# Bias, exponential and s made over both banks of q at once (1024 columns) in tiles 7 to 14 of a retrieval-attention and dense kernel

## What is computed

```
xn  = layernorm(x)
q   = xn @ Wq.T + bq              (one head in four is used: 8 heads x 128 = 1024 columns)
s   = elu(q) + 1                  (= max(q, 0) + exp(min(q, 0)))
a   = s / (sum over the head of s*z + 1e-6)
out = x + (a @ M per head, repeated over 4 heads) @ Wo.T  +  xn @ (w * w_scale) + b
```

## Time and profile before

| | |
|---|---|
| Time, median of 3 runs | 243.72 us (243.49 to 243.82) |
| The profiled execution | 243.56 us, of which the span of the trace is 241.7 us |
| PE busy | 234.1 us, 97% of the span |
| DVE, ACT, POOL busy | 178.0, 119.6 and 108.4 us |
| TensorE clock granted | full speed in every slice |

### The profile page before, as it was taken

One profiled execution on the slowest core, in us unless ns is written; L12 is line 12 of the kernel. 1 busy time (PEld: TensorE's weight loads), 2 busy tenths in 40 slices (PEclk: granted clock), 3 DMA queues, 4 the chain that ended last, 5 costly groups with the idle time before them and its releaser, 6 DMA issues.

```text
span 241.7 us, 3385 instructions
## 1 busy us (share of the span) xinstructions
PE 234.1 (97%) x1030; PEld 186.7 (77%) x1030; DVE 178.0 (74%) x266; ACT 119.6 (49%) x276; POOL 108.4 (45%) x108
## 2 busy tenths in 40 slices
PE   8699999998999999999999999999999999999995
PEld 2488788885776788888888888888888888788885
DVE  2889695897998669887687694958666778995631
ACT  2654626628648923655463526455463747341110
POOL 1058734756271815553434326263403629657500
PEclk9999999999999999999999999999999999999999
DMA  7999999999370211424252515221212223244441
GB/s 225 405 417 411 383 242 225 216 217 217 94 252 5 53 51 52 127 54 126 53 168 53 161 50 169 52 91 42 88 52 73 56 75 108 76 136 136 133 174 44
DMA packets 21985, 34.83 MB, mean 144 GB/s; under 512 B 5200, under 2 KB 13136, under 8 KB 20816
## 3 DMA queue, kind: packets, MB, share of 16 engines
q1 hardware_dynamic: 19344, 26.63, 33.4%
q0 software_dynamic: 1376, 6.82, 13.4%
q10 hardware_dynamic: 1248, 1.18, 1.8%
HBM read 22.02 MB, written 4.19 MB: 108 GB/s over the span
## 4 chain that ended last, share of the span: by engine, by line
PE 33%; issue 31%; POOL 18%; DVE 8%; SPq 4%; DMA 2%; ACT 2%; ACTq 1%; POOLq 0%; DVEq 0%
POOL e_and_sz L313 9%; POOL xT L288 5%; PE attn_ps L793 4%; PE attn_ps L794 4%; PE attn_ps L795 4%; SPq L219 4%; POOL x L321 3%; PE q_ps L793 3%; PE q_ps L795 3%; PE q_ps L794 3%; DVE aT_lo L654 2%; PE dense_ps L793 2%; PE dense_ps L795 2%; PE dense_ps L794 2%; DMA xT<-in_xT 2%
## 5 line engine op out<-in xcount | busy, mean ns | idle before, releaser
L313 POOL TENSOR_TENSOR e_and_sz<-s,z_b 128x512 f32<-128x512 f32 x32 | 42.0, 1340 | 40.3 <-DVE den L633 40.2
L441 ACT ACTIVATE s<-s,rden 128x128 f32<-128x128 f32 x128 | 39.2, 389 | 40.5 <-DVE rden L637 40.5
L793 PE MATMUL attn_ps<-P_hi,aT_hi 128*128 128x512 f32 (+1 forms) x128 | 49.8, 389 | 0.5 <-DVE aT_lo L654 0.5
L795 PE MATMUL attn_ps<-P_hi,aT_lo 128*128 128x512 f32 (+1 forms) x128 | 49.1, 383 | 0.0
L794 PE MATMUL attn_ps<-P_lo,aT_hi 128*128 128x512 f32 (+1 forms) x128 | 49.0, 383 | 0.0
L793 PE MATMUL q_ps<-WqT_hi,xT_hi 128*128 128x512 f32 x104 | 42.1, 405 | 0.3 <-DVE s L628 0.3
L795 PE MATMUL q_ps<-WqT_hi,xT_lo 128*128 128x512 f32 x104 | 40.6, 390 | 0.0
L794 PE MATMUL q_ps<-WqT_lo,xT_hi 128*128 128x512 f32 x104 | 40.5, 389 | 0.0
L288 POOL TENSOR_TENSOR xT<-xT,mean_b 128x512 f32<-128x512 f32 x13 | 18.3, 1408 | 37.8 <-ACT mean_b L390 31.2
L621 DVE SCALAR_TENSOR_TENSOR q_ps<-q_ps,rstd,bq_b 128x512 f32<-128x512 f32 x28 | 21.0, 753 | 19.3 <-PE q_ps L795 19.3
L793 PEld LDWEIGHTS attn_ps<-P_hi,aT_hi 128*128 128x128 f32 x128 | 24.1, 188 | 6.2 <-issue 0.9
(11 more groups left out here) (82 smaller groups left out, 365.3 us busy)
## 6 DMA issues: line engine op xcount, KB each, us to landing
x<-in_WoT POOLq DMA_DIRECT2D x6, 1024.0 KB, 10.6
x<-in_x SPq DMA_DIRECT2D x16, 256.0 KB, 3.9
xT<-in_xT SPq DMA_DIRECT2D x16, 256.0 KB, 4.1
aT<-s SPq DMA_DIRECT2D x124, 32.0 KB, 1.9
out<-x SPq DMA_DIRECT2D x15, 256.0 KB, 2.3
MT<-s SPq DMA_DIRECT2D x96, 32.0 KB, 1.9
x<-in_WoT SPq DMA_DIRECT2D x2, 1024.0 KB, 14.0
s<-in_WqT SPq DMA_DIRECT2D x2, 512.0 KB, 7.1
```

The costliest lines, as they stand in the source:

```text
L313: nc.gpsimd.tensor_tensor(sz_eps[:, :, h * D // 2:(h + 1) * D // 2].rearrange("p g (j c) -> p j g c", j=2), by_quarter(sbuf_s[:, t % SRING ...
L441: last = nc.scalar.activation(a_g, a_g, ACT.Copy, scale=rden[:, t % 2, g:g + 1])
L793: nc.tensor.matmul(out, x_hi, w_hi, start=start, stop=False)
L795: return nc.tensor.matmul(out, x_lo, w_hi, start=False, stop=stop)
```

## The change

The four q banks become one PSUM tensor, whose banks lie side by side. For tiles 7 to 14 one instruction of 1024 columns takes the place of two of 512 for the bias, for each of the two steps of the exponential, and for s. These instructions wait for both halves of q. The places of the other work in the loops move with this: `xT_hi` on ACT comes behind both steps of the exponential instead of between the halves, `xT_lo` on DVE ahead of all of s instead of between its halves, and `moments` ahead of the bias. In step 7 the splits of P come ahead as well. Tile 15 keeps its two halves. PE, POOL and SP keep their lists.

```diff
-        q_ps = [bank(f"q{i}_ps") for i in range(4)]
+        q_banks = ctx.enter_context(nc.psum_tensor("q_ps", [P, 4, 512], F32))
+        q_ps = [q_banks[:, i, :] for i in range(4)]
...
+        def both_banks(t):
+            return q_banks[:, 2 * (t % 2):2 * (t % 2) + 2, :].rearrange("p h n -> p (h n)")
...
+            def exp_of_both(t):
+                act.wait_ge(q_biased, 2 * t + 2)
+                act.wait_ge(s_ready, 2 * t)
+                nc.scalar.activation(ebuf, both_banks(t), ACT.Relu, scale=-1.0).then_inc(qneg_ready, 2)
+                act.wait_ge(qneg_ready, 2 * t + 2)
+                nc.scalar.activation(ebuf, ebuf, ACT.Exp, scale=-1.0).then_inc(exp_ready, 2)
...
             for t in range(LEAD, T):
-                exp_of(t, 0)
-                if t + 1 < T:
-                    copy_xT_hi(t + 1)
                 if t == LEAD:
                     copy_P_hi(6)
-                exp_of(t, 1)
-                if t == LEAD:
                     copy_P_hi(7)
+                if t < T - 1:
+                    exp_of_both(t)
+                    copy_xT_hi(t + 1)
+                else:
+                    exp_of(t, 0)
+                    exp_of(t, 1)
                 copy_aT_hi(t - LEAD + 1)
...
+            def add_bias_to_both(t):
+                dve.wait_ge(rstd_ready, t + 1)
+                dve.wait_ge(q_filled, 2 * t + 2)
+                nc.vector.scalar_tensor_tensor(both_banks(t), both_banks(t), rstd[:, t:t + 1], bq_b[:], ALU.mult, ALU.add
+                                               ).then_inc(q_biased, 2)
+
+            def make_both_s(t):
+                dve.wait_ge(exp_ready, 2 * t + 2)
+                if t >= SRING:
+                    dve.wait_ge(aT_in[in_MT(t - SRING)], aT_landed(t - SRING))
+                nc.vector.scalar_tensor_tensor(sbuf_s[:, t % SRING, :], both_banks(t), 0.0, ebuf, ALU.max, ALU.add
+                                               ).then_inc(s_ready, 2)
...
             for t in range(LEAD, T):
-                add_bias(t, 0)
                 if t == LEAD:
                     split_P_lo(5)
                 if t + 2 < T:
                     moments(t + 2)
-                add_bias(t, 1)
                 if t == LEAD:
                     split_P_lo(6)
-                if t == LEAD:
                     split_P_lo(7)
-                turn_blocks(t - BEHIND - 1)
-                if t == LEAD:
+                if t < T - 1:
+                    add_bias_to_both(t)
+                    turn_blocks(t - BEHIND - 1)
                     split_xT_lo(t + 1)
-                make_s(t, 0)
-                if LEAD < t < T - 1:
-                    split_xT_lo(t + 1)
-                make_s(t, 1)
+                    make_both_s(t)
+                else:
+                    add_bias(t, 0)
+                    add_bias(t, 1)
+                    turn_blocks(t - BEHIND - 1)
+                    make_s(t, 0)
+                    make_s(t, 1)
                 split_aT_lo(t - LEAD + 1)
```

More of the change, by code:

```diff
@@ L95, in q_bank @@
             if t < LEAD and t % 3 == 1:
-                return attn_ps[h]
+                return attn_ps[h][:]
             return q_ps[2 * (t % 3 == 2 if t < LEAD else t % 2) + h]
+        def both_banks(t):
+            return q_banks[:, 2 * (t % 2):2 * (t % 2) + 2, :].rearrange("p h n -> p (h n)")
         def last_attn_ps(c):
-            return [attn_ps[(T - 1) % 2], q_ps[0]][c][:, 0:HID // 2]
+            return [attn_ps[(T - 1) % 2][:, 0:HID // 2], q_ps[0][:, 0:HID // 2]][c]
         x_in = [sem(f"x_in{t}") for t in range(T)]
@@ L427, in exp_of @@
                 e = ebuf[:, halves(h)]
-                nc.scalar.activation(e, q_bank(t, h)[:], ACT.Relu, scale=-1.0).then_inc(qneg_ready, 1)
+                nc.scalar.activation(e, q_bank(t, h), ACT.Relu, scale=-1.0).then_inc(qneg_ready, 1)
                 act.wait_ge(qneg_ready, 2 * t + h + 1)
                 nc.scalar.activation(e, e, ACT.Exp, scale=-1.0).then_inc(exp_ready, 1)
+            def exp_of_both(t):
[4 more added lines that the diff above has]
+                nc.scalar.activation(ebuf, ebuf, ACT.Exp, scale=-1.0).then_inc(exp_ready, 2)
             def copy_P_hi(g):
@@ L620, in add_bias @@
                 dve.wait_ge(q_filled, 2 * t + h + 1)
-                nc.vector.scalar_tensor_tensor(q_bank(t, h)[:], q_bank(t, h)[:], rstd[:, t:t + 1],
+                nc.vector.scalar_tensor_tensor(q_bank(t, h), q_bank(t, h), rstd[:, t:t + 1],
                                                bq_b[:, halves(h)], ALU.mult, ALU.add).then_inc(q_biased, 1)
@@ L627, in make_s @@
                     dve.wait_ge(aT_in[in_MT(t - SRING)], aT_landed(t - SRING))
-                nc.vector.scalar_tensor_tensor(sbuf_s[:, t % SRING, halves(h)], q_bank(t, h)[:], 0.0,
+                nc.vector.scalar_tensor_tensor(sbuf_s[:, t % SRING, halves(h)], q_bank(t, h), 0.0,
                                                ebuf[:, halves(h)], ALU.max, ALU.add).then_inc(s_ready, 1)
+            def add_bias_to_both(t):
[9 more added lines that the diff above has]
+                                               ).then_inc(s_ready, 2)
             def denominator(t):
@@ L805, in q_chunk @@
             def q_chunk(t, h, k):
-                return three_passes(q_bank(t, h)[:], xT_hi[:, t % HRING, k, :], xT_lo[:, t % HRING, k, :],
+                return three_passes(q_bank(t, h), xT_hi[:, t % HRING, k, :], xT_lo[:, t % HRING, k, :],
                                     WqT_hi[:, k, halves(h)], WqT_lo[:, k, halves(h)], k == 0, k == K - 1)
@@ L814, in hi_hi @@
                     pe.wait_ge(wq_hi_ready, 2 * k + h + 1)
-                nc.tensor.matmul(q_bank(t, h)[:], xT_hi[:, t, k, :], WqT_hi[:, k, halves(h)], start=k == 0, stop=False)
+                nc.tensor.matmul(q_bank(t, h), xT_hi[:, t, k, :], WqT_hi[:, k, halves(h)], start=k == 0, stop=False)
             def lo_hi(t, h, k):
@@ L821, in lo_hi @@
                     pe.wait_ge(xT_lo_ready, 1 + k // 2)
-                nc.tensor.matmul(q_bank(t, h)[:], xT_lo[:, t, k, :], WqT_hi[:, k, halves(h)], start=False, stop=False)
+                nc.tensor.matmul(q_bank(t, h), xT_lo[:, t, k, :], WqT_hi[:, k, halves(h)], start=False, stop=False)
             def hi_lo(t, h, k):
@@ L826, in hi_lo @@
                     pe.wait_ge(wq_lo_ready, 2 * k + h + 1)
-                return nc.tensor.matmul(q_bank(t, h)[:], xT_hi[:, t, k, :], WqT_lo[:, k, halves(h)], start=False,
+                return nc.tensor.matmul(q_bank(t, h), xT_hi[:, t, k, :], WqT_lo[:, k, halves(h)], start=False,
                                         stop=k == K - 1)
```

## The result

The changed kernel takes 245.89 us (median of 4, 245.47 to 246.81), the kernel before 243.69 (median of 4, 243.49 to 243.82); the ratio is 1.0096, 95% interval 1.0066 to 1.0126. Run again later, five times on another occasion, it took 245.60 (245.42 to 245.69) and the ratio was 1.0078 (1.0065 to 1.0092). The forecast was 245.6, a loss of 1.88 us. The loss measured is 2.20 by the first medians and 1.98 by the later ones (the kernel before took 243.62 beside them), and both medians lie in the range. Why the first is 0.2 larger is not shown.

What follows compares the result with a forecast made beforehand. PE is busy 234.1 of 241.7 us, but the end hangs on a slackless DVE, ACT and POOL chain from step 14 or 15. 243.56 + 1.87 = 245.43, with the median 0.16 above: 245.6 us, range 244.9 to 246.4.

Steps and rivals of the forecast that it cites:

- No slack in the tail, seven steps for nothing, step 14 for all of it: Steps 7 to 13 hide their delay with 3.4 us slack; the chain from step 14 delays the end one for one.
- The cost of the width: Instructions of 1024 columns cost 0.54 us more for bias and s, 0.45 more for each step of the exponential.
- Late by 2.18 in step 14, by 1.87 behind step 15: aT_lo(8) starts at 183.96 instead of 181.78 us, aT_lo(9) at 196.65 instead of 194.78.
- ACT's list holds s in step 15: Tile 15's exponentials stand behind a of tile 12 on ACT, ending at 196.02 instead of 193.84; s waits until 196.05.
- The rival that had the delay regained there: Step 15: exponentials don't hold s back, only DVE's own 0.46 us goes on, 244.2 us; chance 0.08.
- PE's waits: PE waits 1.4 us at product_attn(10) and about 1.0 before product_attn(11), 2.4 together instead of 0.52.
- the chain of before: Back from product_attn(11) at 211.32: aT_lo(11) 210.16, aT_hi(11) 209.50, ACT's four DMA issues 206.70, waiting for aT_lo(10).
- The rival of DVE and POOL colliding: The shift puts a DVE subtraction on the path beside POOL, costing up to 1.75 us more, 247.3; chance 0.06.
- What the one wait is worth: PE's only wait from 70 us on, 0.52 us for aT_lo; without it at best 243.2 us; faster has chance 0.02.
- One sign of being wrong: The prediction is wrong if the wide instructions are cheaper than 1.22 and 1.06 us.

Runs made afterwards that it cites:

- b_7to13: Kernel before with both banks at once only in tiles 7 to 13, tile 14 in halves as before: 243.57 us, ratio 0.9998 to the kernel before.
- c_only14: Kernel before with both banks at once only in tile 14, tiles 7 to 13 in halves: 245.71 us, ratio 1.0080 to the kernel before.
- d_xthi_first: Changed kernel with the copy xT_hi of the next tile ahead of the exponential on ACT: 244.55 us, ratio 1.0035 to the kernel before.
- f_bias_only: Kernel before with only the bias of both banks at once in tiles 7 to 14: 244.65 us, ratio 1.0041 to the kernel before.
- e_exp15_early: Changed kernel with tile 15's exponentials and aT_hi of tile 9 ahead of a of tile 12 on ACT: 244.61 us, ratio 1.0036 to the kernel before.
- j_addb_early: Kernel before with POOL's additions of b for tiles 9 to 11 moved forward to step 14: 242.97 us, ratio 0.9964 to the kernel before.
- m_7to13_addb_early: Kernel before with both banks at once in tiles 7 to 13 and the additions of b forward: 243.41 us, ratio 0.9984 to the kernel before.
- l_after_addb_early: Changed kernel with POOL's additions of b moved forward to step 14: 244.81 us, ratio 1.0044 to the kernel before.
- n_all_mended: Changed kernel with xT_hi before the exponential, tile 15's exponentials and aT_hi(9) before a of tile 12, additions of b forward: 242.65 us, ratio 0.9957 to kernel before.

## Why the prediction was right

- **No slack in the tail, seven steps for nothing, step 14 for all of it.** Shown by the pair b_7to13 and c_only14, 0.9998 and 1.0080.
- **The cost of the width.** Measured within 0.02 us of each of the four values. The rows of other instructions of 1024 columns were good enough, across two PSUM banks too.
- **Late by 2.18 in step 14, by 1.87 behind step 15.** 2.25 and 1.88 in the profile, with its start taken off, and 1.85 at product 11. d_xthi_first and f_bias_only gave 0.9 and 0.9 to 1.0 where the same way of working through the lists gave 0.75 and 1.0.
- **ACT's list holds s in step 15.** Shown by e_exp15_early. The rival that had the delay regained there needed just this edit; it came to 0.9 and not to its 0.46. `aT_lo(9)` was 0.77 late there: 0.58 stood ahead of s, since the second bias ran that much later, and 0.19 came in s itself, whose second half waited for its exponential (ACT ends it at 195.25, s follows at 195.29).
- **PE's waits** were foretold as 1.4 and 1.0 and measured as 1.68 and 0.53. Their sum is 2.2 against 2.4. Two things were off. The sum took 24 matmuls of 0.225 off the end of the last one, 210.80, but the rows of neighbouring matmuls overlap; product 10 started at 205.19 and not at 205.4. For the same reason, and since PE starts again slower than its pace (below), product 10 takes 5.72 us to its end behind the wait and not 5.4, so its successor waits less.
- **A step of the argument that was false** without harm to the sum: the chain of before as I told it had ACT's four DMA issues as the link that holds `aT_lo(11)`. The issues let the subtraction start at 210.16, and by itself its first half would have ended 0.67 later; POOL's addition of b, which the prediction has nowhere on the path, ran until 210.62 and held that end until 211.18. Since all of it hangs on `aT_lo(10)`, the shift was the same by either link. With the addition gone and nothing else changed, the first half would by estimate have ended at 210.16 + 0.67 = 210.83, when PE is ready at 210.80; no run made that edit alone, since in j_addb_early `aT_lo(10)` was 1.1 us earlier too.
- **The rival of DVE and POOL colliding** brought nothing new on the path of the changed kernel: `aT_lo(10)` and `(11)` take 3.00 and 1.61 there, as before. But these collisions were on the path all along, and m_7to13_addb_early lost half its gain by a new one, 1.0 us at one subtraction.
- **What the one wait is worth** was put too low, at half a microsecond (243.2 at best). Without it j_addb_early is 0.86 us faster, for the reason given below.
- **One sign of being wrong was set against the forecast itself:** it names a step of the exponential cheaper than 1.06, where 1.05 was expected and 1.03 came. It has no bearing on the time.

## What to carry to other kernels

On an engine that waits for PE, a half that is worked on while PE makes the other half costs no time; merging the halves saves busy time (here 4.4 and 2.8 us) and moves all of the work behind PE's last matmul. Look for the one step whose delay reaches the end, here the last one ahead of the tail, and judge the change there alone. Before moving an instruction of an idle engine, look at what it runs beside: moving the same four additions gained 0.9 us in the kernel before, and only 0.4 where they ran 2 us later and met a subtraction.

## What was not expected of the hardware

**PE loses more than the wait shows.** In the kernel before, PE's rows around the wait of 0.52 (start, duration):

```profile
210.41 0.39 PE L795 MATMUL attn_ps<-P_hi,aT_lo 128*128 128x512 f32 x1
211.32 0.47 PE L793 MATMUL attn_ps<-P_hi,aT_hi 128*128 128x512 f32 x1 [0.52 <-DVE aT_lo L654]
211.63 0.39 PE L794 MATMUL attn_ps<-P_lo,aT_hi 128*128 128x512 f32 x1
211.86 0.39 PE L795 MATMUL attn_ps<-P_hi,aT_lo 128*128 128x512 f32 x1
```

Without a wait a matmul starts every 0.23 us, though its row lasts 0.39, so neighbouring rows overlap. Two matmuls behind 210.41 one would start at 210.87; it starts at 211.63, 0.76 later. The wait shows 0.52 of this. 0.16 are missing because the idle time is counted from the end of a row, which would have overlapped the next, and 0.08 because the first matmul behind the wait is followed after 0.31 and not 0.23. So a wait costs some 0.25 us more than its row says. It fits the gains of j_addb_early (0.86 us by the medians, for a wait of 0.52) and l_after_addb_early (0.8, for 0.53 to 0.58). The clock was granted in full at each of these waits.

**DVE's subtraction of two SBUF tiles beside POOL.** `xT_lo` of 512 columns took 0.67 us alone and 1.71 and 1.03 when POOL was adding; `aT_lo` 1.28 for two halves and up to 3.0. Each time the held half ended 0.55 to 0.58 behind the end of a POOL instruction: in m_7to13_addb_early POOL's last addition ends at 181.99 and `xT_lo` at 182.54, in n_all_mended 181.05 and 181.61, in j_addb_early `times_z` at 204.67 and the first half of `aT_lo(10)` at 205.22, and `aT_lo(11)` above. The Trainium skill (SBUF — State Buffer, Who interferes with whom) has the ports that VectorE and GpSimd share as an exclusive lock, says that a VectorE instruction with two SBUF inputs contends with a GpSimd instruction that reads SBUF, and that the order of issue decides who is blocked. These rows agree, and in both directions. Behind a subtraction that was already waiting or running POOL is held too: its addition at 204.32 took 1.74 us beside `aT_lo(10)` (1.73 in the changed kernel), where others took 1.30. In m_7to13_addb_early the subtraction began while POOL's last addition was running, and the four additions took 5.05 us, against 5.04 without a subtraction beside them.
